# Level outputs of a gated slot attention on parts of the TensorE array, in one group, with a new order of the engines

## What is computed

```python
h = hidden_states
q, k, v, w = (short_conv(h @ W, c) for W, c in ((Wq, cq), (Wk, ck), (Wv, cv), (Ww, cw)))
g = log_sigmoid(h @ Wf1 @ Wf2)
w = l2norm(w)                                   # per head
def step(carry, xs):                            # over the 512 positions
    Sk, Sv = carry
    q_t, k_t, v_t, w_t, g_t, b_t = xs
    gt = exp(g_t)
    bw = b_t[:, :, None] * w_t
    Sk = Sk * gt[:, :, None, :] + k_t[..., :, None] * bw[:, :, None, :]
    Sv = Sv * gt[..., None] + bw[..., None] * v_t[:, :, None, :]
    s = einsum('bhd,bhdm->bhm', q_t, Sk) * SCALE
    a = softmax(s, axis=-1)
    o_t = einsum('bhm,bhmd->bhd', a, Sv)
o = o * rsqrt(mean(o * o) + EPS) * norm_w * sigmoid(gate)
return o.reshape(...) @ Wo
```

## Time and profile before

| | us |
|---|---|
| median of 3 runs | 2795.52 (2793.87 to 2795.84) |
| the profiled execution | 2791.86 |
| its span | 2790.1 |
| TensorE busy | 2741.3 (98%) |
| VectorE busy | 2247.3 (81%) |
| ScalarE busy | 1629.7 (58%) |
| GpSimd busy | 1420.1 (51%) |

### The profile page before, as it was taken

How to read it: one execution, slowest core, us unless ns; L and a number is a source line. 1 busy time by engine, 2 the same in 40 slices (tenths; PEclk the granted TensorE clock), 3 DMA queues, 4 the chain that set the end, 5 groups by cost and what they waited for, 6 DMA issues and landing times. The chain is left out here.

```text
span 2790.1 us, 42861 instructions
## 1 busy us (share of the span) xinstructions
PE 2741.3 (98%) x13558; PEld 1910.1 (68%) x13558; DVE 2247.3 (81%) x5841; ACT 1629.7 (58%) x3649; POOL 1420.1 (51%) x2122
## 2 busy tenths in 40 slices
PE   6999899999999999999999999999999999999999
PEld 5888566666666666666666666666666666666887
DVE  7554689988888999888889998888898999884543
ACT  5111676677666666776666767666766666661110
POOL 0200366666666666665666666656666666661000
PEclk9999999999999999999999999999999999999999
DMA  4500211111112111111121111111211111105000
GB/s 170 196 16 16 79 35 36 35 50 35 49 35 65 55 61 35 50 35 50 35 73 50 58 35 50 35 50 35 80 50 58 35 51 37 50 29 193 16 16 31
DMA packets 90929, 151.03 MB, mean 54 GB/s; under 512 B 9296, under 2 KB 30928, under 8 KB 90192
## 3 DMA queue, kind: packets, MB, share of 16 engines
q1 hardware_dynamic: 90704, 148.29, 16.7%
HBM read 127.02 MB, written 21.23 MB: 53 GB/s over the span
## 5 line engine op out<-in xcount | busy, mean ns | idle before, releaser
L946 POOL TENSOR_TENSOR s<-s,tmp 128x256 f32<-128x256 f32 (+1 forms) x448 | 358.8, 801 | 312.0 <-DVE tmp L1258 276.1
L1611 PE MATMUL ps<-rows_even,standing 128*128 128x512 f32 x1024 | 498.1, 595 | 2.7 <-ACTq L1062 2.7
L1611 PE MATMUL ps<-hT,standing 128*128 128x512 f32 x1024 | 497.4, 593 | 0.0
L946 POOL TENSOR_TENSOR X<-S,D 128x256 f32<-128x256 f32 x384 | 278.8, 726 | 97.2 <-ACT S L1121 73.2
L1654 PEld LDWEIGHTS ps<-Y,S 128*128 128x128 f32 x1536 | 221.3, 191 | 153.1 <-issue 135.5
L946 POOL TENSOR_TENSOR Y<-aT,D 128x256 f32<-128x256 f32 x384 | 280.3, 751 | 0.0
L341 ACT ACTIVATE sig<-up_ps 128x512 f32<-128x512 f32 x88 | 52.6, 597 | 389.8 <-PE up_ps L570 389.8
L946 POOL TENSOR_TENSOR A<-ident,dg 128x512 f32<-128x512 f32 x64 | 66.7, 1041 | 380.3 <-DVE standing L1348 356.9
L1642 PEld LDWEIGHTS ps<-AM,XT 128*128 128x128 f32 x1536 | 211.6, 191 | 64.1 <-issue 60.2
L1258 DVE TENSOR_TENSOR tmp<-ps,D 128x256 f32<-128x256 f32 (+1 forms) x448 | 196.2, 438 | 63.7 <-PE ps L1642 47.6
L1587 PE MATMUL ps<-standing,og 128*128 128x512 f32 x480 | 245.2, 593 | 0.0
(11 more groups left out here) (215 smaller groups left out, 6679.5 us busy)
## 6 DMA issues: line engine op xcount, KB each, us to landing
standing<-in_wk_dram SPq DMA_DIRECT2D x64, 256.0 KB, 2.5
standing<-in_ww_dram SPq DMA_DIRECT2D x64, 256.0 KB, 2.6
standing<-in_wq_dram SPq DMA_DIRECT2D x64, 256.0 KB, 2.7
standing<-in_wv_dram SPq DMA_DIRECT2D x64, 256.0 KB, 2.8
standing<-in_wo_dram SPq DMA_DIRECT2D x64, 256.0 KB, 3.3
wq_dram<-wq SPq DMA_DIRECT2D x3, 2816.0 KB, 20.0
space<-in_w_dram SPq DMA_DIRECT2D x8, 704.0 KB, 11.1
x_sb<-in_x_dram SPq DMA_DIRECT2D x4, 1024.0 KB, 5.6
```

The lines of the kernel that those rows point to most:

```text
L946: return nc.gpsimd.tensor_tensor(out, in0, in1, op)
L1611: mm = nc.tensor.matmul(bank[x][:, :], ck_(slot[x], kk), hT[n // NH % 2][:, kk, :], start=(kk == 0), stop=(kk == KT - 1))
```

## The change

1. `outputs` no longer multiplies all 128 source columns with 128 target columns. For levels 1 to 32 it takes 32 sources at a time (32 columns of the array, `source_parts`) with the 32 targets of the same blocks (`target_part`), eight matmuls a level; for level 64 it takes 64 with 64, four matmuls. The results go to the PSUM partitions of those sources. What is left out of each product are entries that the mask never took.
2. Two levels share a bank, each with one half of its columns, and the merge of the first waits for the outputs of both.
3. `S[1]`, `S[2]`, `S[4]`, `S[8]` are held twice, by turns.
4. All seven `outputs` stand together, after the last projection of v. The seven merges stand together behind `ss`.
5. The rest of all four engines' orders is rearranged: among other steps the first output row comes before v, the second before the transposes of k, and `chunk_scores` after `chunk_outputs`; `scores(4)` comes earlier; ScalarE copies the first decays before the halves of w; GpSimd makes `Y[64]` and `Yst` right after `Y[32]` and S[1] last.

```diff
-PE_EARLY = "k w g q wT v x2T kT A x4T x8T vT x16T x32T gate x64T xbT s0 s2 U0 U1 s4 s8 U2".split()
+PE_EARLY = "k w g q wT v x2T kT A x4T vT x8T x16T x32T gate x64T s4 xbT s0 s2 s8 U2 U0 U1".split()
...
+TWICE = (1, 2, 4, 8)
...
+def source_parts(l):
+
+    width = P // 2 if l == 64 else P // 4
+    return [(p0, p0 + width) for p0 in range(0, P, width)]
+
+
+def target_part(t, l, i, j, rows=(0, P)):
+
+    if l == 64:
+        return rows_pat(t, *rows, j * P + i * (P // 2), (1, P // 2))
+    if l == 32:
+        return rows_pat(t, *rows, (j % 2) * P + i * (P // 2) + (j // 2) * (P // 4), (1, P // 4))
+    return rows_pat(t, *rows, i * (P // 2) + j * (P // 8), (P, 2), (1, P // 8))
...
-        S = {l: sb(f"S{l}", [P, HALF]) for l in LEVELS}
+        S = [{l: sb(f"S{l}", [P, HALF]) for l in LEVELS}]
+        S += [S[0] | {l: sb(f"S{l}b", [P, HALF]) for l in TWICE}]
...
+        for l, (i, half) in {1: (0, 0), 2: (0, 1), 4: (1, 0), 8: (1, 1), 16: (5, 0), 32: (5, 1), 64: (6, 0)}.items():
+            bank[f"a2_{l}"] = psum[i][:, half * HALF:(half + 1) * HALF]
...
                 def outputs(l, done):
                     for i in range(2):
-                        last = nc.tensor.matmul(pair_columns(bank[f"a2_{l}"], i), ck_(S[l], i),
-                                                odd_targets(aT, i) if l == 1 else pair_columns(Y[l], i),
-                                                start=True, stop=True)
+                        for j, (p0, p1) in enumerate(source_parts(l)):
+                            last = nc.tensor.matmul(target_part(bank[f"a2_{l}"], l, i, j, (p0, p1)),
+                                                    ck_(S[u % 2][l], i)[:, p0:p1],
+                                                    odd_target_part(aT, i, j) if l == 1 else target_part(Y[l], l, i, j),
+                                                    start=True, stop=True)
                     last.then_inc(done, 1)
...
                     dve.wait_ge(act_early, after(ACT_EARLY, "sq", n))
                     nc.vector.tensor_reduce(ss[:, :], sq[:, :, :], AX.X, ALU.add).then_inc(dve_early, 1)
...
+                if late:
+                    dve.wait_ge(pe_late, after(PE_LATE, "a2_2", u))
+                    merge(1)
+                    dve.wait_ge(dve_late, after(DVE_LATE, "a2_1", u))
+                    merge(2)
+                    dve.wait_ge(pe_late, after(PE_LATE, "a2_8", u))
+                    dve.wait_ge(dve_late, after(DVE_LATE, "a2_2", u))
+                    merge(4)
+                    dve.wait_ge(dve_late, after(DVE_LATE, "a2_4", u))
+                    merge(8)
+                    dve.wait_ge(pe_late, after(PE_LATE, "a2_32", u))
                     dve.wait_ge(dve_late, after(DVE_LATE, "a2_8", u))
                     merge(16)
```

More of the change, by code:

```diff
@@ L687, in odd_targets, with rows_pat, odd_target_part @@
     return pat(t, 1 + i * P, (HALF - 1, 2), (2, P // 2))
+def rows_pat(t, p0, p1, at, *dims):
+    part = t[p0:p1, :]
+    return bass.AP(part.tensor, part.offset + at, [list(part.ap[0])] + [list(d) for d in dims])
+def source_parts(l):
[7 more added lines that the diff above has]
+    return rows_pat(t, *rows, i * (P // 2) + j * (P // 8), (P, 2), (1, P // 8))
+def odd_target_part(t, i, j):
+    return pat(t, 1 + i * P + j * (P // 4), (HALF - 1, 2), (2, P // 8))
 def level_one(t):
@@ L1036, in turn @@
                     tt(r2[:, :], r1[:, :], oss[:, :]).then_inc(pool_late, 1)
+                if early:
+                    pool.wait_ge(act_early, after(ACT_EARLY, "c32", n))
+                    decay_sources(32)
+                if late:
                     pool.wait_ge(pool_late, after(POOL_LATE, "r2", u))
                     tt(r3[:, :], r2[:, :], rms_eps[:, :], ALU.add).then_inc(pool_late, 1)
+                if early:
+                    pool.wait_ge(act_early, after(ACT_EARLY, "c64", n))
+                    pool.wait_ge(dve_early, after(DVE_EARLY, "p64", n))
+                    decay_sources(64)
+                if late:
                     pool.wait_ge(pool_late, after(POOL_LATE, "r3", u))
@@ L1136, in turn @@
                                          ACT.Copy).then_inc(act_late, 1)
-                if late:
-                    if late:
-                        act.wait_ge(dve_late, after(DVE_LATE, "og", u - 1))
+                    act.wait_ge(dve_late, after(DVE_LATE, "og", u - 1))
                     nc.scalar.activation(sg[:, :], bank["gate"][:, :], ACT.Sigmoid,
@@ L1152, in turn @@
                 if early:
[L1153 removed]
                     if n == 0:
                         act.wait_ge(small_full, 16 * SMALL)
+                    act.wait_ge(pe_early, after(PE_EARLY, "k", n))
                     first_tap("k")
+                if n == 0:
+                    first_low_rank(0)
                 if late:
@@ L1229, in turn @@
                     keep_sources(64)
+                    act.wait_ge(pe_early, after(PE_EARLY, "x8T", n))
+                    pair_rows(8)
                     act.wait_ge(act_early, after(ACT_EARLY, "h64", n))
@@ L1466, in turn @@
                 if early:
-                    dve.wait_ge(dve_early, after(DVE_EARLY, "p4", n))
-                    decays(4)
+                    dve.wait_ge(act_early, after(ACT_EARLY, "acc_v", n))
+                    conv("v", 1)
                     dve.wait_ge(act_early, after(ACT_EARLY, "h8", n))
@@ L1628, in transpose_sources, with transpose_into_upper @@
                 def transpose_sources(l, done):
-                    transpose(f"x{l}T", lambda i: ck_(S[l], i), done, 2)
+                    transpose(f"x{l}T", lambda i: ck_(S[n % 2][l], i), done, 2)
+                def transpose_into_upper(into):
+                    for c in range(2, C):
+                        nc.tensor.transpose(ck_(into, c), ident[:, :], ident[:, :])
                 def chunk_scores(done):
@@ L1683, in turn @@
                 if late:
-                    pe.wait_ge(dve_early, after(DVE_EARLY, "am32", u))
-                    scores(32, pe_late)
                     pe.wait_ge(act_late, after(ACT_LATE, "sk", u))
@@ L1732, in turn @@
                 if early:
-                    pe.wait_ge(dve_early, after(DVE_EARLY, "ck3", n))
                     if n == 0:
                         pe.wait_ge(act_edge, after(ACT_EDGE, "f1", 0))
+                    pe.wait_ge(dve_early, after(DVE_EARLY, "ck3", n))
                     project_low("g", f1T[n // NH % 2])
                     project("q", 2)
+                    project("q", 3)
+                if n == 0:
+                    low_rows(0, 0)
+                    transpose_into_upper(psum[5])
+                    low_rows(0, 1)
+                if u >= C:
+                    out_rows(u - C, bank["out"], 0)
+                if early:
+                    pe.wait_ge(dve_early, after(DVE_EARLY, "cw3", n))
+                    project("v", 0)
+                    project("v", 1)
+                    project("v", 2)
+                    pe.wait_ge(act_early, after(ACT_EARLY, "w", n))
+                    transpose("wT", lambda c: ck_(w, c), pe_early)
+                    if n == 0:
+                        second_low_rank(0)
+                    project("v", 3)
                 if late:
@@ L1820, in turn @@
                     transpose_sources(64, pe_early)
+                    pe.wait_ge(dve_early, after(DVE_EARLY, "vr", n))
+                    scores(4, pe_early)
                     pe.wait_ge(act_early, after(ACT_EARLY, "xt16", n))
```

378 lines of the change are left out of this document (162 added, 216 removed), and 6 rows, old and new, of the table bank.

## The result

The changed kernel took 2915.72 us (median of 4 runs, 2910.37 to 2919.15), the kernel before 2794.69 us beside it (4 runs, 2793.60 to 2795.84): ratio 1.0431, 95% interval 1.0413 to 1.0449. That is 121 us slower; 68 were predicted. The profiled execution has a span of 2915.5 us.

The account below looks back on a forecast made before the run. TensorE, busy 98%, bounds the kernel; afterwards the merge chain sets the turn. A turn grows from 34.14 to 35.3 us; 60 turns at 1.13 us add 68 us, giving 2863 us, range 2760 to 2955.

Parts of the forecast that it names:

- TensorE's group: The seven levels' outputs on TensorE, 104 load-and-matmul pairs at 0.028 us: 2.9 us a turn, from 0.7 to 11.4 us.
- My lower end, 0.7 us: Level-output group on TensorE if four parts of the array run side by side, 0.007 us a pair.
- my alternative drain: Draining TensorE at three tiling-mode changes a turn: 0.36 us each, 1.1 us a turn, group 4.0 us; not in the sum.
- Inputs of the group in time: Before the level-output group: ScalarE's and GpSimd's inputs are ready, so the group, starting at 1415.15, waits for nothing.
- The merge wait: Before the chunk outputs: seven merges in a row on VectorE take 4.4 us, so TensorE stands still 1.3 us a turn.
- One sign: Expected in the profile: VectorE's merge group shows idle time before it, released by itself.
- VectorE has some 15 us of work between the last merge and the next turn, by its own steps, so it keeps up: Behind the chunk outputs: VectorE does not delay TensorE, except s4 by perhaps 0.2 us, left out.
- 17.07 us: TensorE work from the chunk outputs to the next turn: 17.04 less 0.86 (output row) plus 0.89 (chunk scores).
- The fast case: Rival: merges keep their spacing among other work and parts overlap; a turn is 33.5 us, 2755 us; chance 0.22.
- Payment by the instruction: Rival: level-output pairs cost 0.055 us, the group 5.7 us, a turn 36.7 us, 2947 us in all; chance 0.15.
- The clock: Rival: stalls lower TensorE's granted clock; 2908 us if every second turn, 2953 us if every turn; chance 0.13.
- Nothing: Rival: chain and work balance, a turn stays at 34.1 us, 2795 us; chance 0.05.

Follow-up runs that it names:

- e1: Kernel before with only the level outputs multiplied in parts, old order and single S buffers kept: 2789.62 us, ratio 0.9984.
- e3: Changed kernel without the predicated copies (merges) of levels 16 and 32: 2867.93 us, ratio 1.0264 to the kernel before.
- e4: Changed kernel with GpSimd's S1 product and X products of levels 32 and 64 cut to a few elements from the third unit on: 2827.46 us, ratio 1.0119.
- e7b: Kernel before with three more GpSimd products a turn where it was idle, written to buffers nothing reads: 2824.93 us, ratio 1.0110.

## Why the prediction was right in sign and short in size

- **TensorE's group: mis-sized, from the wrong row.** I took 0.028 us a pair from the four-column matmuls, 2.9 us. A pair is one weight load and one matmul instruction; with 32 columns pairs start 9.5 ns apart, near my bound for parts that run side by side, and the whole group with its mode changes takes 1.71 us. My lower end, 0.7 us, lacked the switches; my alternative drain of 0.36 us a change, 1.1 us a turn, was twice too much: the group is 0.54 us longer than its six levels of 0.155 and four 64-wide matmuls of 0.24 us in all, and e1's six groups pay 0.3 us each. The Trainium skill's up to 4x (TensorEngine Tiling (Array Packing), Theoretical Speedup) came to three: a level took 0.45 us whole, 0.15 us in parts.
- **Inputs of the group in time: right.** It started 12.57 us into the turn; I had 12.54.
- **The merge wait: right in place and cause, size a little short.** 1.57 us a turn was measured against 1.3, 63 times. The chain of seven takes 4.2 us (1476.52 to 1480.70), 4.4 predicted. Because the group is short, it starts 13.14 us into the turn and not 13.7, so the chunk outputs start at 17.38 us, not 18.2. e3 confirms the chain as the bound: two merges less, 0.72 us less. One sign failed: the merges were to show idle time released by themselves, and the whole run has 0.4 us of it. Each gap is some 0.1 us; it shows as spacing, four steps from 1478.16 to 1480.26, 0.53 us for an instruction of 0.44. By this half alone the turn would have been 34.4 us, 0.28 more than before.
- **"VectorE has some 15 us of work between the last merge and the next turn, by its own steps, so it keeps up": this step failed.** I took VectorE's durations as fixed while the new orders put GpSimd's products beside its masks. From the last merge to the next turn VectorE was busy 15.0 of 17.7 us before (1419.03 to 1436.75), as I had it, and 16.3 of 18.7 us after (1480.70 to 1499.38). That still leaves room in the sum; what came too late was one product, `kv` at 1487.38, 24.0 us into the turn and 23.2 in e4. Behind the chunk outputs I had 17.07 us, measured were 18.62. e4 gives 1.49 us of the difference back; e7b makes 0.46 us of the same kind in the kernel before. This one item, 94 us over 63 turns, is larger than the whole predicted loss. That 2863 us came as near to 2916 as it did is luck: the 0.8 us a turn that I had too much in the first half hid half of the 1.55 us that I lacked in the second.
- **Rivals.** The fast case fell, though its premises half held: the parts do run side by side, but the merges pay their gaps. Payment by the instruction fell: 9.5 ns, not 55 (and its sum, 36.7 us a turn, gives 2949 us, not 2947). The clock did not fall: 1.00 in mid-stage, 0.995 over the run. "Nothing" fell.

## What to carry to other kernels

When an order table moves one engine's work, lay the timelines of VectorE and GpSimd over each other in the new order: where a VectorE product with both operands in SBUF meets a large GpSimd product, the one that comes second is longer by most of what is left of the other (a mask of 0.41 us took 0.83). Where TensorE is busy 98% of the time, look how close the others stand behind it before counting on its savings; here parts that saved 1.9 us a turn, less some 1.1 us of switches, were worth 0.15 us. Narrow matmuls on parts of the array are cheap once grouped, so that the entry and the exit are paid once, but the group must not turn the engine that consumes it into a chain with nothing between its links.

## What the runs showed of the hardware that I had not expected

- Float32 matmul instructions of 32 stationary and 32 moving columns on four parts of the array start 9.5 ns apart, weight loads included; sixteen, which are eight matmuls, in 0.15 us (1475.95 to 1476.10).
- Going into such a group and out again costs some 0.3 us (six groups in e1), 0.20 us at least around a single level, 0.54 us for the changed kernel's one group with its step from 32 to 64 columns.
- VectorE's masks of 0.41 us took 0.83 and 0.85 us beside a GpSimd product, and GpSimd's product of 0.745 us 0.92 to 0.96 us beside VectorE's; instructions with an operand in PSUM kept their length (0.68 us). Beside GpSimd's power over four elements, 1.15 us long, a diagonal kept its 0.29 us.
- Seven predicated copies that wait for each other start 0.53 us apart from the third on, at 0.44 us each; among other work the next instruction starts 0.34 us after one (before, 1414.61 to 1414.95).
